# The whole copy of x ahead of expert 0, and layer 1 begun on half of a slot tile

## What is computed

```
probs = jax.nn.softmax(xf @ gate_w.T, axis=-1)
scores_sel = _xmoe_route(probs)
h = jax.nn.gelu(jnp.einsum('nd,efd->enf', xf, w1), approximate=False)
y_e = jnp.einsum('enf,edf->end', h, w2)
y = jnp.einsum('ne,end->nd', scores_sel, y_e)
...
x = x + y
```

## Time and profile before

| | us |
|---|---|
| median of 3 runs | 266.07 |
| lowest, highest | 265.47, 266.68 |
| the profiled execution | 268.34 |
| its span, first to last instruction | 266.5 |
| PE busy in the span | 244.1 |
| DVE busy | 198.7 |
| ACT busy | 149.4 |
| POOL busy | 138.5 |

### The profile page before, as it was taken

One profiled execution on the slowest core, in us unless ns is written; L12 is line 12 of the kernel. 1 busy time (PEld: TensorE's weight loads), 2 busy tenths in 40 slices (PEclk: granted clock), 3 DMA queues, 4 the chain that ended last, 5 costly groups with the idle time before them and its releaser, 6 DMA issues.

```text
span 266.5 us, 4044 instructions
## 1 busy us (share of the span) xinstructions
PE 244.1 (92%) x1449; PEld 185.2 (69%) x1449; DVE 198.7 (75%) x433; ACT 149.4 (56%) x275; POOL 138.5 (52%) x105
## 2 busy tenths in 40 slices
PE   7787888889999969999999999999999999999970
PEld 2455532236998848888888888888878888888750
DVE  5285889998989399977997799689779966933230
ACT  4631038874566377746864775587468658734100
POOL 1000000027871687787578848766885771487530
PEclk9997999999999999999999999999999999999995
DMA  6999999726467978779648956974894690372621
GB/s 232 423 420 412 486 350 404 215 68 193 118 199 301 332 227 214 166 128 303 185 47 236 242 115 93 323 175 73 184 275 135 78 221 17 42 82 40 178 94 39
DMA packets 12787, 53.78 MB, mean 202 GB/s; under 512 B 2768, under 2 KB 3152, under 8 KB 9552
## 3 DMA queue, kind: packets, MB, share of 16 engines
q1 hardware_dynamic: 4512, 35.68, 37.2%
q0 software_dynamic: 8256, 17.85, 32.7%
HBM read 44.74 MB, written 18.22 MB: 236 GB/s over the span
## 4 chain that ended last, share of the span: by engine, by line
PE 62%; DVE 13%; DMA 12%; POOL 5%; issue 4%; SPq 1%; ACT 1%; POOLq 0%; DVEq 0%
PE bank L831 9%; PE bank L833 9%; PE bank L832 9%; PE bank L846 9%; PE bank L847 9%; PE bank L851 9%; DMA region<-in_xt 7%; DMA w2raw<-in_w 5%; DVE region L690 4%; PE bank L813 4%; POOL xg L296 2%; POOL region L296 2%; POOL score L304 1%; PE bank L900 1%; DMA score<-probs_scratch,pidx 1%
## 5 line engine op out<-in xcount | busy, mean ns | idle before, releaser
L312 POOL DMA_INDIRECT out<-ysb,scat x32 | 64.3, 2010 | 44.3 <-ACT ysb L390 27.3
L508 DVE SCALAR_TENSOR_TENSOR w1rot<-w1raw,rot,w1rot 128x512 f32<-128x512 f32 x84 | 63.2, 752 | 5.2 <-ACT w1rot L350 3.2
L831 PE MATMUL bank<-w2h,hh 128*128 128x512 f32 x128 | 51.5, 402 | 0.0
L833 PE MATMUL bank<-w2h,hl 128*128 128x512 f32 x128 | 50.1, 391 | 0.0
L832 PE MATMUL bank<-w2l,hh 128*128 128x512 f32 x128 | 50.0, 390 | 0.0
L296 POOL DMA_INDIRECT xg<-in_x,gath x16 | 17.6, 1100 | 61.2 <-DVE gath L558 56.7
L846 PE MATMUL bank<-xh,w1h 128*128 128x512 f32 x112 | 44.0, 393 | 0.0
L847 PE MATMUL bank<-xh,w1l 128*128 128x512 f32 x112 | 43.6, 390 | 0.0
L537 DVE TENSOR_TENSOR hl<-hf,hh 128x512 fp32r<-128x512 f32 x32 | 22.0, 689 | 25.3 <-ACT hh L381 25.3
L377 ACT ACTIVATE hf<-bank 128x512 f32<-128x512 f32 x32 | 19.1, 596 | 34.6 <-PE bank L851 31.7
L304 POOL DMA_INDIRECT score<-probs_scratch,pidx x32 | 33.1, 1035 | 9.7 <-issue 9.4
(11 more groups left out here) (144 smaller groups left out, 374.5 us busy)
## 6 DMA issues: line engine op xcount, KB each, us to landing
region<-in_xt SPq DMA_DIRECT2D x8, 1024.0 KB, 10.0
w1raw<-in_w SPq DMA_DIRECT2D x8, 1024.0 KB, 11.9
w2raw<-in_w SPq DMA_DIRECT2D x8, 1024.0 KB, 8.4
score<-probs_scratch,pidx POOLq DMA_INDIRECT x32, 4.9
out<-ysb,scat POOLq DMA_INDIRECT x32, 6.0
probs_scratch<-probs SPq DMA_DIRECT2D x1, 384.0 KB, 24.0
ch<-in_ch SPq DMA_DIRECT2D x1, 320.5 KB, 10.7
xg<-in_x,gath POOLq DMA_INDIRECT x16, 3.8
```

What stands on the lines that cost most here:

```text
L312: pool.indirect_dma_start(out_d, bass.IndirectOffsetOnAxis(scat[:, e, s:s + 1], 0), ysb[:, s, :], None, compute_op=ALU.add if e < LAST els ...
L508: ins = nc.vector.scalar_tensor_tensor(dst, w1raw[:, e % 2, i, :], rot[:, j, i:i + 1], dst, ALU.mult, ALU.add)
L831: nc.tensor.matmul(dst, ah, bh, start=first, stop=False)
L833: return nc.tensor.matmul(dst, al, bh, start=False, stop=last)
```

## The change

The copy of x is made whole, in two DMAs (all rows, then the spare rows), where its first piece was: ahead of the scratch copy of the probabilities. SP's wait for the scores falls away, and POOL waits for two DMAs.

For expert 0, slot tile 1 is transposed in two halves of two parts each, of which the second goes to bank 5; ACT and DVE take each half with its own instruction, and the first half of layer 1 waits for the first half of the tile before its first matmul and for the second before its fifth. The signals of the transposes are five and not four, and the counts of later waits change accordingly (`X0`). Tiles 2 and 3 are transposed after the first half of layer 1, both together; `count_before(1, 2, E)` follows them, `slot_rows(2)` goes behind the third half. ACT does `x_high0(2)`, `x_high0(3)`, `rows_out(1, 2, E)` and `w1_first(1, 0)` after `hidden(0, 0)`. DVE does `count_tokens(2, E)` after `x_low0(1)`, `x_low0(2)` and `x_low0(3)` after the first `h_low`, then `slots_after(2)`, and `slot_tables(2)` behind the second `h_low`, ahead of `rotate_w1(1, 1)`. One `keep_clock` has 4 matmuls for 5, and a `keep_clock(1)` stands ahead of the first half of layer 1.

```diff
+X0_PARTS = ((slice(0, C4),), (slice(0, 2), slice(2, C4)), (slice(0, C4),), (slice(0, C4),))
+X0_DONE = ((1,), (2, 3), (4,), (5,))
+X0 = X0_DONE[-1][-1]
...
-        x0bank = lambda s: bank[(0, 1, 4, 5)[s]][:, :].rearrange("p (c n) -> p c n", c=C4)
+        x0bank = lambda s, js: bank[5 if js.start else (0, 1, 4, 5)[s]][:, :].rearrange("p (c n) -> p c n", c=C4)
...
                 if e == 1:
-                    sp.wait_ge(xt_mm, S4)
+                    sp.wait_ge(xt_mm, X0)
...
-            sp.dma_start(out_d[0:EARLY, :], x_d[0:EARLY, :]).then_inc(out_base, 16)
+            sp.dma_start(out_d[0:N, :], x_d[0:N, :]).then_inc(out_base, 16)
+            sp.dma_start(out_d[N:N + SPARE, :], x_d[0:SPARE, :]).then_inc(out_base, 16)
             sp.wait_ge(prob_ready, len(CHUNKS))
             sp.dma_start(probs_d.rearrange("(p n) o -> p (n o)", p=P),
                          probs[:, :, :].rearrange("p t e -> p (t e)")).then_inc(probs_out, 16)
-            sp.wait_ge(score_in[0], 16 * S4)
-            sp.dma_start(out_d[EARLY:N, :], x_d[EARLY:N, :]).then_inc(out_base, 16)
-            sp.dma_start(out_d[N:N + SPARE, :], x_d[0:SPARE, :]).then_inc(out_base, 16)
...
             def x_high0(s):
-                act.wait_ge(xt_mm, s + 1)
-                nc.scalar.activation(xh[:, :, s * P:(s + 1) * P], x0bank(s), ACT.Copy).then_inc(x_hi, 1)
+                for done, js in zip(X0_DONE[s], X0_PARTS[s]):
+                    act.wait_ge(xt_mm, done)
+                    nc.scalar.activation(xh[:, js, s * P:(s + 1) * P], x0bank(s, js)[:, js], ACT.Copy).then_inc(x_hi, 1)
...
             x_high0(0)
             x_high0(1)
-            rows_out(1, 2, E)
-            x_high0(2)
-            w1_first(1, 0)
             for e in range(E):
                 more = e + 1 < E
                 hidden(e, 0)
                 if e == 0:
+                    x_high0(2)
                     x_high0(3)
+                    rows_out(1, 2, E)
+                    w1_first(1, 0)
...
             w1_low(0, 3, C4)
-            count_tokens(2, E)
             x_low0(0)
             x_low0(1)
-            x_low0(2)
-            slots_after(2)
+            count_tokens(2, E)
             w2_low(0)
...
                 h_low(e, 0)
                 if e == 0:
+                    x_low0(2)
                     x_low0(3)
-                    slot_tables(2)
+                    slots_after(2)
                     rotate_w1(1, 0)
                 elif more:
                     rotate_w1(e + 1, 1)
                 h_low(e, 1)
+                if later:
+                    slot_tables(e + 2)
                 if e == 0:
                     rotate_w1(1, 1)
-                elif later:
-                    slot_tables(e + 2)
...
             def transpose_x0(s):
 
                 pe.wait_ge(xg_in[0][s], 16)
-                for j in range(C4):
-                    last = nc.tensor.transpose(x0bank(s)[:, j, :], xg[0][:, s, j * P:(j + 1) * P], ident)
-                last.then_inc(xt_mm, 1)
+                for js in X0_PARTS[s]:
+                    for j in range(C4)[js]:
+                        last = nc.tensor.transpose(x0bank(s, js)[:, j, :], xg[0][:, s, j * P:(j + 1) * P], ident)
+                    last.then_inc(xt_mm, 1)
...
-                if n % 2 == 0:
-                    pe.wait_ge(x_hi, S4 // 2 * (1 + n // 2))
+                if n == 0:
+                    pe.wait_ge(x_hi, X0_DONE[1][0])
+                if n == 2:
+                    pe.wait_ge(x_hi, X0)
...
                     for j in range(C4):
+                        if n == 0 and i == 0 and j == 2:
+                            pe.wait_ge(x_hi, X0_DONE[1][1])
...
-            keep_clock(5, nbank)
+            keep_clock(4, nbank)
...
             keep_clock(3, cbank[1])
             transpose_x0(1)
-            count_before(1, 2, E)
-            transpose_x0(2)
+            keep_clock(1, cbank[1])
             for e in range(E):
                 if e == 0:
                     layer1_half(0)
+                    transpose_x0(2)
                     transpose_x0(3)
-                    slot_rows(2)
+                    count_before(1, 2, E)
                     layer1_half(1)
                     layer1_half(2)
+                    slot_rows(2)
                     layer1_half(3)
```

More of the change, by code:

```diff
@@ L54 @@
 SPARE = CAP
-EARLY = 7 * N // 8
 NEPS = 1e-8
@@ L293, in gather_x @@
                 if e >= 2:
-                    pool.wait_ge(xt_mm, C4 * (e - 1))
+                    pool.wait_ge(xt_mm, X0 + C4 * (e - 2))
                 for s in range(S4):
@@ L315, in gather_sums @@
             def gather_sums():
-                pool.wait_ge(xt_mm, C4 * LAST)
+                pool.wait_ge(xt_mm, X0 + C4 * (LAST - 1))
                 for k in range(S4):
@@ L333, in _ @@
                 if e == 0:
-                    pool.wait_ge(out_base, 48)
+                    pool.wait_ge(out_base, 32)
                 for s in range(S4):
@@ L364, in x_high @@
             def x_high(e, j):
-                act.wait_ge(xt_mm, C4 * e + j + 1)
+                act.wait_ge(xt_mm, X0 + C4 * (e - 1) + j + 1)
                 nc.scalar.activation(xh[:, j, :], xbank[j % 2][:, :], ACT.Copy).then_inc(x_hi, 1)
             def x_high0(s):
-                act.wait_ge(xt_mm, s + 1)
-                nc.scalar.activation(xh[:, :, s * P:(s + 1) * P], x0bank(s), ACT.Copy).then_inc(x_hi, 1)
+                for done, js in zip(X0_DONE[s], X0_PARTS[s]):
+                    act.wait_ge(xt_mm, done)
+                    nc.scalar.activation(xh[:, js, s * P:(s + 1) * P], x0bank(s, js)[:, js], ACT.Copy).then_inc(x_hi, 1)
             def hidden(e, f):
@@ L524, in x_low @@
             def x_low(e, j):
-                dve.wait_ge(x_hi, C4 * e + j + 1)
+                dve.wait_ge(x_hi, X0 + C4 * (e - 1) + j + 1)
                 nc.vector.tensor_tensor(xl[:, j, :], xbank[j % 2][:, :], xh[:, j, :].bitcast(FP32),
@@ L529, in x_low0 @@
             def x_low0(s):
-                dve.wait_ge(x_hi, s + 1)
-                nc.vector.tensor_tensor(xl[:, :, s * P:(s + 1) * P], x0bank(s), xh[:, :, s * P:(s + 1) * P].bitcast(FP32),
-                                        ALU.subtract).then_inc(x_lo, 1)
+                for done, js in zip(X0_DONE[s], X0_PARTS[s]):
+                    dve.wait_ge(x_hi, done)
+                    last = nc.vector.tensor_tensor(xl[:, js, s * P:(s + 1) * P], x0bank(s, js)[:, js],
+                                                   xh[:, js, s * P:(s + 1) * P].bitcast(FP32), ALU.subtract)
+                last.then_inc(x_lo, 1)
             def h_low(e, f):
@@ L844, in layer1 @@
                     if f == 0:
-                        pe.wait_ge(x_hi, C4 * e + j + 1)
+                        pe.wait_ge(x_hi, X0 + C4 * (e - 1) + j + 1)
                     nc.tensor.matmul(dst, w1h[e % 2][:, j, fs], xh[:, j, :], start=(j == 0), stop=False)
```

## The result

The changed kernel took 269.24 us (median of 4 runs, 268.75 to 269.72) against 265.88 for the kernel before: 1.0105 times as long, with a 95% interval of 1.0064 to 1.0147. The forecast was 265.5 us and a range of 263.9 to 267.3. Ratios are those on record, which leave out the few executions over 1.5% above the fastest of their kernel, and they are not simply the quotient of the two medians.

What follows compares the result with a forecast made beforehand. PE, busy 92% of the span, was taken as the bound, with one 2.5 us stall from SP's order. Terms -2.52 + 1.7 + 0.2 - 0.1 + 0.15 = -0.57 gave 267.8 us profiled, 265.5 median, range 263.9 to 267.3.

Steps and rivals of the forecast that it cites:

- The clock: Rival at the start of expert 0: TensorE's clock falls while PE waits for gathers, costing 1.7 us; chance 0.12.
- Part 1: Load of w2 of expert 1 no longer waits for the copy, so PE's stall before slot_rows(3) goes: -2.5 us.
- Part 2: Start of expert 0: the longer early copy holds the gathers of slot tiles 0 and 1 to its end: +1.7 us.
- The first rival: Gathers slip through between pieces of the copy, delaying tile 1 by 0 to 0.9 us: 264.2 us; chance 0.28.
- Parts 3, 4 and 5: Expert 0: layer 1 on half of slot tile 1, +0.2 us; one dummy matmul fewer, -0.1; DVE and ACT order, +0.15.
- part 5: Layer 2 of expert 0: DVE's later tables delay the rotation chain to y_out(0, 1), stalling PE: +0.15 us, bounds 0 and 1.2.

Runs made afterwards that it cites:

- e12: The kernel before, unchanged, run a third time: 267.28 us, 1.0004 of before; its profiled execution took 266.04 us.
- e5: The changed kernel, unedited, measured again over 12 runs: 269.97 us, 1.0064 of before.
- e1: The kernel before, unchanged, profiled a second time: 268.20 us in four runs, 1.0107 of before.
- e3: The changed kernel with the copy of x back in its three old pieces and places, leaving the new order and half tile: 266.21 us, 1.0004 of before.
- e4: The changed kernel with 7/8 of the copy early and the rest behind the loads of w2 of expert 1 and w1 of expert 2: 264.70 us, 0.9942 of before.
- e8: e4 with slot tile 1 transposed and converted whole instead of in halves: 265.41 us, 0.9888 of before.
- e9: The kernel before, old order, with the copy's last eighth and spare rows behind the loads of w2 of expert 1 and w1 of expert 2: 264.53 us, 0.9943.
- e11: The same kernel as e4, measured again: 264.93 us, 0.9960 of before.
- e6: The changed kernel with 26 dummy matmuls instead of 8 between slot_rows(1) and the first transposes: 268.90 us, 1.0036 of before.
- e10: The changed kernel with its copy made in pieces of 8 KB instead of 64 KB: 268.88 us, 1.0089 of before.
- e2: The kernel before with the whole copy ahead of the probabilities and nothing else changed: 268.28 us, 1.0070 of before.
- e13: The changed kernel with the scratch copy of the probabilities issued only after the gather of slot tile 1 landed: 268.37 us, 1.0067 of before.

## Why the prediction was wrong

Against the profile it was worked out from, the prediction was nearly right: it said 267.8 us for a profiled execution, and that of the changed kernel took 268.75, about the clock's price more. The forecast of the median, 265.5, missed by 3.7 us, mostly because the difference between that profile and the median, 2.3 us, was carried over. The terms come out only between executions of the same kind.

The account can be made between two executions without the fall near 21 us, e12 (span 264.2) and the profile after (266.9), +2.7 us. The medians of the first runs differ by 3.4; the profile after is the fastest of its four, and one in which the clock was low for 3.4 us and not, as in e5, for 6.8. Transposes of slot tile 0: 60.03 to 63.28, +3.25. From there to layer 1: 3.56 against 3.39 us; with 1.11 us moved out of it, +0.94. The stall: -1.45. Sum +2.74.

**Part 1, the stall: right in kind, wrong in size.** It is gone, in the changed kernel and in every kernel whose load of w2 goes early, and the load was issued at 71.47 as forecast. But in the traces other than the first it was worth 1.2 to 1.5 us. The 2.52 came from a single execution, in which SP issued the load 1.7 us later than in e1, and e1, e3 and e12 don't repeat it. Error of this term: 1.1 us.

**Part 2, the hold of the gathers: right in kind and in place, wrong in size, and this is the step that failed most.** I said that the gathers are held to the copy's end and that tile 0 would be there at 63.3; PE began on it at 63.28. (The copy landed at 61.7, outside my 62.3 to 63.9, and the gather followed after 1.5 us and not after 0.2; the two errors cancelled, which is luck.) The failing step is what I subtracted: "PE begins its transposes 1.8 us late". I measured from 61.47, in a profile whose front part was late, to a moment that the copy fixes. The six traces without the fall whose gathers aren't held (e12, e3, e4, e8, e9, e11) have tile 0 at 59.9 to 60.1, and of the 25 runs of before beside e1, 20 have a mean clock of 0.987 or more, above that of the first profile (0.982) and of e1 (0.985). In such an execution the hold costs 3.3 us. The sentence where it went wrong is "the profile is 2.3 above it before any change, and I carry the difference over". A difference of the front part can be carried over only while the front part sets the time. Here the copy took that over, and the delay that I thought common to both kernels was in before alone. Error: 1.5 us. The page of the profile showed it: a clock of 7 in the fourth slice, used as a price in a rival and not as a sign that this execution wasn't typical.

**The clock: a rival that happened.** I put the point at a wait of 2.5 us, gave it 0.12, and expected a wait of 2.0. The wait was 3.69, again because the front part ends earlier than shown, and the clock fell 2.5 to 3.7 us into it, where waits of 2.46 and 2.52 us passed without a fall. It cost 0.9 us in the profile and 1.8 in e5; my price was 1.7.

**The first rival** (gathers slip through) had 0.28, and half of the range below the forecast came from it. By the rule of the Trainium skill (DMA: Bandwidth & Descriptors, section on queues, rings and completion order), each engine alternates between its queues a packet at a time. I took one piece of the copy for a packet, and that is the step that failed here: pieces of 8 KB should then have let the gathers pass, and they didn't (63.42 us). The same section of the Trainium skill says that a packet is typically 9 to 17 descriptors and at most 64, which is not what the profile counts as a packet. If a piece is one descriptor, which no trace here shows, the nine pieces of 64 KB that each engine had in the changed kernel (9.44 MB by 16 engines), or 9 to 17 pieces of 8 KB at 0.3 to 0.5 us (an estimate of 3 to 8 us), can be a single packet. So the traces speak against my reading of the rule; they don't decide against the rule.

**Parts 3, 4 and 5: small, as forecast.** Handing over and order come to about zero: e3 is at 1.0004, and from the transposes of tile 0 to layer 1 e11 needs 2.49 us (59.97 to 62.46), with the 1.11 moved out 3.60, against 3.56 in e12; I had 0.2 (the clock being at its upper level in both; e6, in which tile 1 was there already, needs 2.19 us, 3.30 with the 1.11). The first gather is issued 0.3 us earlier in the changed kernel than in e12; I had 0.1. For part 5 I had a wait of 0.15 in layer 2 of expert 0; none of PE's matmuls waits there in the changed kernel, where expert 0 is late as a whole. Where it isn't late there is a wait, of 0.27 and 0.26 us in e4 and e11, but also of 0.71 in e9 with the old order, and its cause is a held gather of scores and not my chain of rotations on DVE. My reason for it doesn't stand.

**The rest.** Errors of 1.5 (the hold), 1.1 (stall) and 0.9 (clock), less some 0.3 for parts 3 and 5, make 3.2 us; the forecast was a gain of 0.6, the account a loss of 2.7. What stays open: why the scores came later and SP's issue took longer in the first profile, what brings the fall of the clock near 21 us, and why before had a median of 268.41 beside e5 to e8 and not 266.

## What to carry to other kernels

A transfer that fits exactly in front of another is not a free place: before more is put there, work out when it ends in absolute time, on its slowest DMA engine, and compare that with the earliest moment in a typical execution at which the next one is wanted. If the profiled execution is slower than the median, find where (here a row of the clock told it) before a sum is made from it, since only what sets the time in both kernels can be carried over. And move the load that is waited for ahead of a bulk copy rather than the copy ahead of everything: e9, which moves the last two pieces of the copy behind two loads, gave 0.994 of before. What is moved behind a load can hold the next gather too: look there as well.

## What the hardware showed

A gather on POOL's queue, issued while a copy from HBM to HBM was running on SP's queue, moved nothing while sixteen pieces of the copy were under way, with pieces of 64 KB (first packet at 59.63, 3.4 us after the issue, against 1.8 with no copy) and of 8 KB (first packet at 60.03). In the changed kernel it landed only after the last four pieces, which ended 1.3 us or more behind the other twelve: 7.0 us from issue to landing against 3.6. In e4, e9 and e11 a gather of scores beside two loads and the rest of the copy took 10.4 to 10.5 us against 2.8.

In a wait of 3.7 us TensorE's clock went to its lower level 2.5 us (e5), 3.0 us (e10) or 3.7 us (the profile after) after PE had become idle, and stayed there for 3.4 or 6.8 us. It didn't fall in waits of 2.46 (e2), 2.16 (e13) or 2.52 us (before).
